# Row maxima of attention: products sent one by one, one transpose a set, rows spread through DRAM, the second set's done in the projection

## The reference

```python
q, k, v = (proj(w_q), proj(w_k), proj(w_v))        # 32 heads of 16, 4 batches of 512 tokens
scores = jnp.einsum('bhqd,bhkd->bhqk', q, k) / jnp.sqrt(jnp.float32(D_K))
attn = jax.nn.softmax(scores, axis=-1)
out = jnp.einsum('bhqk,bhkd->bhqd', attn, v)
```

## Time and profile before

| | us |
|---|---|
| median of 3 runs | 1923.91 (1920.84 to 1927.97) |
| profiled run | 1923.31 |
| its span | 1921.6 |
| mean granted clock of TensorE | 0.961 |
| projection, from the first rows gathered | about 744 to 921.6 |
| attention | 922 to 1327 |
| busy: PE, DVE, ACT, POOL | 1718.2, 1475.6, 829.8, 680.0 |

### The profile page before, as it was taken

The page is one execution under the profiler, slowest core; times in us unless marked ns, Lnnn a source line. Parts: engine busy times, 40 slices in busy tenths (PEclk is TensorE's granted clock), DMA queues, the critical chain, the costliest instruction groups (busy, mean ns, idle before and its releaser), DMA issues. The chain is left out here.

```text
span 1921.6 us, 24417 instructions
## 1 busy us (share of the span) xinstructions
PE 1718.2 (89%) x7762; PEld 1045.0 (54%) x7762; DVE 1475.6 (77%) x2715; ACT 829.8 (43%) x1415; POOL 680.0 (35%) x413
## 2 busy tenths in 40 slices
PE   8999979786959995999788888888989999999997
PEld 2333323224747873876333333334768778778786
DVE  7999999999726666753588888884976776776678
ACT  6657464444203554321477777776521111111112
POOL 5898999994234654300130000000031330330100
PEclk8999999999979997999799999999989999999999
DMA  5434344321147996864543333320010000000002
GB/s 159 122 124 119 117 129 123 91 71 39 67 185 281 414 414 244 278 213 159 138 119 91 91 93 94 94 72 4 1 67 1 33 34 1 34 33 1 1 1 88
DMA packets 111583, 213.27 MB, mean 111 GB/s; under 512 B 19012, under 2 KB 35780, under 8 KB 110554
## 3 DMA queue, kind: packets, MB, share of 16 engines
q1 hardware_dynamic: 106337, 194.94, 31.3%
q0 software_dynamic: 5120, 16.78, 2.6%
HBM read 146.85 MB, written 62.72 MB: 109 GB/s over the span
## 5 line engine op out<-in xcount | busy, mean ns | idle before, releaser
L2150 DVE TENSOR_REDUCE early_top<-att_first 128x1 f32<-128x512 f32 x480 | 311.4, 686 | 52.5 <-PE att_first L2035 45.0
L562 DVE TENSOR_TENSOR_SCAN ssm_h<-ssm_da,ssm_dbx 128x512 f32<-128x512 f32 x256 | 303.8, 1206 | 1.8 <-ACT ssm_da L441 1.5
L283 POOL TENSOR_TENSOR ssm_dbx<-ssm_u,ssm_bbc 128x2048 f32<-128x2048 f32 x63 | 285.6, 4534 | 26.2 <-DVE ssm_h L562 25.7
L2111 ACT ACTIVATE att_prob<-att_second 128x1024 f32<-128x1024 f32 x256 | 248.1, 1022 | 82.8 <-PE att_second L2055 77.7
L653 PE MATMUL ssm_y<-ssm_hc,all_ident 128*128 128x512 f32 x384 | 216.1, 646 | 42.4 <-DVE ssm_hc L528 42.4
L441 ACT ACTIVATE ssm_da<-ssm_dt,ssm_minus_a 128x512 f32<-128x512 f32 x256 | 176.6, 690 | 168.2 <-DVE ssm_h L562 168.1
L2533 ACT ACTIVATE ffn_silu<-ffn_pg 128x256 f32<-128x256 f32 x112 | 43.2, 386 | 407.1 <-PE ffn_pg L129 407.1
L2398 POOL TENSOR_TENSOR pairs_raw<-pairs_raw,pairs_scales 128x512 f32<-128x512 f32 x42 | 42.2, 1043 | 485.3 <-DMA pairs_raw<-in_w 485.3
L127 PE MATMUL ffn_pg<-pairs_wh,last_XH 128*128 128x512 f32 x448 | 176.9, 395 | 1.7 <-PEq L2201 1.7
L128 PE MATMUL ffn_pg<-pairs_wl,last_XH 128*128 128x512 f32 x448 | 176.8, 395 | 0.0
L129 PE MATMUL ffn_pg<-pairs_wh,last_XL 128*128 128x512 f32 x448 | 175.6, 392 | 0.0
(11 more groups left out here) (355 smaller groups left out, 3635.0 us busy)
## 6 DMA issues: line engine op xcount, KB each, us to landing
all_X<-in_w SPq DMA_DIRECT2D x29, 769.0 KB, 10.3
ssm_bbc<-brow_dram SPq DMA_DIRECT2D x64, 256.0 KB, 4.2
ssm_cbs<-crow_dram SPq DMA_DIRECT2D x64, 256.0 KB, 3.4
sorted_x<-ssm_zero SPq DMA_DIRECT2D x47, 256.0 KB, 3.6
sorted_y<-exp_y SPq DMA_DIRECT2D x47, 256.0 KB, 10.6
mlps_raw<-in_w SPq DMA_DIRECT2D x14, 769.0 KB, 9.5
pairs_raw<-in_w SPq DMA_DIRECT2D x7, 1536.0 KB, 6.5
v_dram<-all_sums SPq DMA_DIRECT2D x16, 512.0 KB
```

What stands on the lines that cost most here:

```text
L283: nc.gpsimd.tensor_tensor(dbx[:, n % 2], u[:, n // STATE % 2], bbc[:, n % RING, :].unsqueeze(1).to_broadcast([P, KC, NB]), ALU.mult).then_ ...
L562: nc.vector.tensor_tensor_scan(h[:, n % 2, c, :], da[:, i % 2, :], dbx[:, n % 2, c, :], 0.0, ALU.mult, ALU.add).then_inc(h_ready, 1)
L2111: nc.scalar.activation(prob[step % 2][:, js, :], p_second[second_place(step, pair) % 2][:], ACT.Exp, scale=DK ** -0.5).then_inc(exp_done, 1)
L2150: nc.vector.tensor_reduce(top[w % 2][:, qt, item:item + 1], p_first[first_place(m) % FIRSTS][:], AX.X, ALU.max).then_inc(max_done, 1)
```

## The change

Five things, all in the way of the maxima:
- *Single products.* In attention `first` sends one product, which waits for its own buffer. A step is now: product 0, `weigh`, turn, products 1 and 2, first pair of scores, product 3, second pair of scores.
- *One transpose.* `minus` is transposed as a whole, 128 x 32 to 32 x 128, and copied as such (32 x 128 instead of 8 x 512).
- *Through DRAM.* SP stores this 16 KB to `max_dram`, waits for the store, and loads it with four DMAs (two partition groups, two head pairs) into the q slot. The six loads of q for set s+4 stand between the store and the four loads; those of k and v come after.
- *Second set in the projection.* Minus after units 36 and 44, turn after units 37 and 45 in the banks of the x transposes, copy after units 38 and 46, store one unit later, the four loads another unit later (for the second set after the last store). In attention turning starts with the third set (`EARLY_SETS`). The waits for stores and loads at the end of the projection are moved to the places in attention that need them; buffers `hi` and `lo` live on and hold the output copies and two slots of v.
- *GpSimd's split* of the output weights is cut into four pieces each.

The diff, cut; left out are the counts of sets and semaphores that follow from this, and blank lines.

```diff
@@ -1461,12 +1461,19 @@
-def load_row_maxima(queue, slot, rows, done):
+def store_row_maxima(queue, g, w, rows, done):
+    queue.dma_start(g.max_dram[w % 2], rows[:].bitcast(F32)).then_inc(done, 16)
+def load_row_maxima(queue, g, slot, w, done):
+    src = g.max_dram[w % 2].rearrange("(t r) q -> r t q", r=2 * SET)
     for k in range(2):
         at = k * ROWS + TERMS
-        queue.dma_start(slot[at:at + 2 * SET, :, :].bitcast(F32),
-                        rows[:].bitcast(F32).unsqueeze(1).to_broadcast([2 * SET, PAIRS, NB])).then_inc(done, 16)
+        for pair in range(PAIRS):
+            queue.dma_start(slot[at:at + 2 * SET, pair, :].bitcast(F32).rearrange("r (t q) -> r t q", q=P), src
+                            ).then_inc(done, 16)
@@ -1569,17 +1580,21 @@
-        FIRST_UNIT, TURN_UNIT = 28, 38
+        FIRST_UNIT = 28
+        MINUS_UNIT = [FIRST_UNIT + QTILES * PAIRS * (w + 1) for w in range(2)]
+        ROWS_UNIT = [u + 2 for u in MINUS_UNIT]
...
             for kind, k in entries:
                 out.append((kind, k))
+                if kind == "unit" and k in MINUS_UNIT:
+                    out.append(("minus", MINUS_UNIT.index(k)))
+                if kind == "unit" and k - 1 in MINUS_UNIT:
+                    out.append(("turn", MINUS_UNIT.index(k - 1)))
                 if kind == "unit" and FIRST_UNIT <= k < FIRST_UNIT + f.STEPS * PAIRS:
                     out.append(("first", k - FIRST_UNIT))
-                if (kind, k) == ("unit", TURN_UNIT):
-                    out.append(("turn", 0))
@@ -1607,9 +1630,10 @@
-                if u == TURN_UNIT + 2:
-                    sp.wait_ge(rows_ready, 1)
-                    load_row_maxima(sp, f.qs[0], f.rows, f.rows_in)
+                if u - 1 in ROWS_UNIT:
+                    send_maxima(ROWS_UNIT.index(u - 1))
+                if u - 2 in ROWS_UNIT:
+                    spread_maxima(ROWS_UNIT.index(u - 2))
@@ -1627,13 +1651,10 @@
-            for k in range(2):
-                sp.wait_ge(stored[k], 16 * qk_before(len(units)))
-                sp.wait_ge(v_stored[k], 16 * TILES // 2)
-            for loaded in f.loaded:
-                sp.wait_ge(loaded, 192)
-            sp.wait_ge(f.selected, 32 * f.LOADED)
-            sp.wait_ge(f.rows_in, 32)
+            if ROWS_UNIT[1] + 1 >= len(units):
+                send_maxima(1)
+            if ROWS_UNIT[1] + 2 >= len(units):
+                spread_maxima(1)
@@ -1707,23 +1728,20 @@
-                if p == TURN_UNIT - FIRST_UNIT + 1:
-                    pe.wait_ge(rows_ready, 1)
...
-            def turn_max(_):
-                pe.wait_ge(minus_lo, 1)
-                pe.wait_ge(max_done, 2 * (TURN_UNIT - FIRST_UNIT + 1))
-                for qt in range(QTILES):
-                    mm = pe.transpose(p_first[0][0:2 * SET, qt * P:(qt + 1) * P],
-                                      minus[:, qt].rearrange("p k h -> p (k h)").bitcast(F32), g.ident[:])
-                mm.then_inc(max_turned, 1)
+            def turn_max(w):
+                pe.wait_ge(minus_lo, w + 1)
+                pe.wait_ge(xl_ready, TILES)
+                pe.transpose(pt[w][0:QTILES * 2 * SET, 0, :], minus[w][:].rearrange("p t k h -> p (t k h)").bitcast(F32),
+                             g.ident[:]).then_inc(max_turned, 1)
@@ -1771,9 +1789,10 @@
-                    if k == TURN_UNIT + 1:
-                        act.wait_ge(max_turned, 1)
-                        nc.scalar.activation(f.rows[:], p_first[0][0:2 * SET, :], ACT.Copy).then_inc(rows_ready, 1)
+                    if k in ROWS_UNIT:
+                        w = ROWS_UNIT.index(k)
+                        act.wait_ge(max_turned, w + 1)
+                        nc.scalar.activation(f.rows[w][:], pt[w][0:QTILES * 2 * SET, 0, :], ACT.Copy).then_inc(rows_ready, 1)
                     continue
@@ -1971,23 +1995,42 @@
-            slot = w % RING
             if w >= RING:
                 sp.wait_ge(pv_done, STEPS * (w - RING + 1))
-            for which, dst in enumerate((qs, ks)):
-                load_terms(sp, g, dst[slot], w, which, loaded[slot])
+            load_terms(sp, g, qs[w % RING], w, 0, loaded[w % RING])
+        def load_rest(sp, w):
+            load_terms(sp, g, ks[w % RING], w, 1, loaded[w % RING])
             load_v(sp, w)
+        def send_max(sp, w):
+            sp.wait_ge(rows_ready, turned_by(w))
+            spread(sp, w - 2)
+            store_row_maxima(sp, g, w, rows[w % 2], f.rows_out)
+        def spread(eng, w):
+            if row_loads(w):
+                eng.wait_ge(m_in[w % RING], 64 * row_loads(w))
+            else:
+                eng.wait_ge(f.rows_in[w], 64)
         def load_max(sp, w):
-            sp.wait_ge(rows_ready, w)
-            load_row_maxima(sp, qs[w % RING], rows[w % 2], m_in[w % RING])
+            sp.wait_ge(f.rows_out, 16 * (w + 1))
+            load_row_maxima(sp, g, qs[w % RING], w, m_in[w % RING])
         @block.sync
         def _(sp):
+            for k in range(2):
+                sp.wait_ge(f.v_stored[k], 16 * TILES // 2)
@@ -1996,10 +2039,14 @@
-                if s + 1 < SETS:
+                if EARLY_SETS <= s + 1 < SETS:
+                    send_max(sp, s + 1)
+                if s + RING - 1 < SETS:
+                    load(sp, s + RING - 1)
+                if EARLY_SETS <= s + 1 < SETS:
                     load_max(sp, s + 1)
                 if s + RING - 1 < SETS:
-                    load(sp, s + RING - 1)
+                    load_rest(sp, s + RING - 1)
@@ -2019,34 +2066,35 @@
-            def first(step, pair):
-                w, qt = step // STEPS, step % STEPS
-                if step % STEPS == 0 and pair == 0 and loads(w):
-                    pe.wait_ge(loaded[w % RING], 192 * loads(w))
-                for k in range(2):
-                    m = 4 * step + 2 * pair + k
-                    first_free(first_place(m))
-                for k in range(2):
-                    m = 4 * step + 2 * pair + k
-                    at = slice(k * ROWS, k * ROWS + TERMS)
-                    pe.matmul(p_first[first_place(m) % FIRSTS][:], qs[w % RING][at, pair, qt * P:(qt + 1) * P],
-                              ks[w % RING][at, pair, :], start=True, stop=True).then_inc(first_ready, 1)
...
+            def first(step, item):
+                w, qt, pair, k = step // STEPS, step % STEPS, item // 2, item % 2
+                if step % STEPS == 0 and item == 0:
+                    if loads(w):
+                        pe.wait_ge(loaded[w % RING], 192 * loads(w))
+                    else:
+                        pe.wait_ge(f.loaded[w], 192)
+                m = 4 * step + item
+                first_free(first_place(m))
+                at = slice(k * ROWS, k * ROWS + TERMS)
+                pe.matmul(p_first[first_place(m) % FIRSTS][:], qs[w % RING][at, pair, qt * P:(qt + 1) * P],
+                          ks[w % RING][at, pair, :], start=True, stop=True).then_inc(first_ready, 1)
...
             def turn_max(w):
-                pe.wait_ge(minus_lo, w)
+                pe.wait_ge(minus_lo, turned_by(w))
                 second_free(maxima_place(w))
-                for qt in range(STEPS):
-                    mm = pe.transpose(p_second[maxima_place(w) % 2][0:2 * SET, 0, qt * P:(qt + 1) * P],
-                                      minus[w % 2][:, qt].rearrange("p k h -> p (k h)").bitcast(F32), g.ident[:])
-                mm.then_inc(max_turned, 1)
+                pe.transpose(p_second[maxima_place(w) % 2][0:QTILES * 2 * SET, 0, 0:P],
+                             minus[w % 2][:].rearrange("p t k h -> p (t k h)").bitcast(F32), g.ident[:]).then_inc(max_turned, 1)
...
             def second(step, pair):
                 s, kt = step // STEPS, step % STEPS
-                if kt == 0 and pair == 0 and row_loads(s):
-                    pe.wait_ge(m_in[s % RING], 32 * row_loads(s))
+                if kt == 0 and pair == 0:
+                    spread(pe, s)
@@ -2084,16 +2132,21 @@
-                if step + LEAD < TOTAL:
+                ahead, more = step + LEAD < TOTAL, step + 1 < TOTAL
+                if ahead:
                     first(step + LEAD, 0)
                 if step:
                     weigh(step - 1)
-                if kt == 1 and s + 1 < SETS:
+                if kt == 1 and EARLY_SETS <= s + 1 < SETS:
                     turn_max(s + 1)
-                if step + LEAD < TOTAL:
+                if ahead:
                     first(step + LEAD, 1)
-                if step + 1 < TOTAL:
+                    first(step + LEAD, 2)
+                if more:
                     second(step + 1, 0)
+                if ahead:
+                    first(step + LEAD, 3)
+                if more:
                     second(step + 1, 1)
@@ -2112,11 +2165,10 @@
-                act.wait_ge(max_turned, w)
-                if w >= 3:
-                    act.wait_ge(m_in[(w - 2) % RING], 32 * row_loads(w - 2))
```

(20 more changed lines are left out.)

86 lines of the change are left out of this document (54 added, 32 removed).

## The result

| | before | after |
|---|---|---|
| median | 1924.93 us (1920.84 to 1927.97, 4 runs) | 1895.65 us (1893.78 to 1898.94, 4 runs) |
| ratio, 95% interval | | 0.9853 (0.9837 to 0.9869) |
| span of the profiled run | 1921.6 | 1892.9 |
| mean granted clock | 0.961 | 0.965 |

29 us, 1.5%, are gone; 1905 was forecast, in a range of 1886 to 1934. To see where, I cut each trace at the first exponential of a set (L2111 before, L2164 after): up to that of set 0, from there to set 3, on to set 31, and to the end.

A forecast was written before the change was run, and what follows sets the result against it. It took a loop through VectorE and TensorE in attention to set the pace. 1923.3 - 2.8 (projection) - 12.7 (start of attention) - 26 x (12.30 - 12.18) (steady sets) = 1904.7, forecast 1905 us, range 1886 to 1934.

The forecast's parts named there:

- The loop through VectorE and TensorE: Attention: maximum, freed product, V products, next product, maximum set the pace; 2.80 us per step, 12.34 per set against 12.30 seen.
- Projection, -2.8: End of the projection: 3.4 us of waiting at the transposes goes, two added transposes cost 0.3 each; sum -2.8.
- Start, -12.7: Start of attention: waits for the second set's maxima and GpSimd's subtraction go, 39.0 us become 26.3; bounds -10 to -13.
- what is late next: Start of attention, once its two waits are gone: the low clock of the first ten us (0.50), which stays.
- Steady sets, the engines: Steady attention: shorter turn (0.53 to 0.20) and 0.13 less per step from single products allow 11.5 us a set.
- Rival 3: Steady attention: splitting costs TensorE more, a set takes 12.5 or 12.6, total 1913 to 1916 us; chance 0.12.
- Steady sets, the way through DRAM: Steady attention: the maxima's detour is the wait the change adds; 4.75 + 0.60 + 6.83 makes a set 12.18 us.
- C: Steady attention: time from the maxima being copied to their use, through store and loads; 6.8 us, bounds 6.15 and 8.2.
- Rival 1: Steady attention: the way through DRAM is short enough, the loop rules at 11.5 to 11.97 a set, 1887 to 1899; chance 0.20.
- the objection that I drew from the page: Way through DRAM: two DMAs in a row at about 2.0 us fixed each, 4.0 plus issue, speak against the change.
- the forecast's case: Whole kernel: both early stages gain as summed and a steady set takes 12.18 us, giving 1905; chance 0.42.
- The chance of faster, 0.67: Whole kernel: chance of a median under 1914.3 us, mostly from the forecast's case (0.38) and Rival 1 (0.20).

The follow-up runs named there:

- weights_apart: Changed kernel with the 1 MB and 1.5 MB weight loads for GpSimd cut into 4 and 6 pieces over several sets; 1871.85 us, ratio to before 0.9838.
- after_again: The changed kernel itself, with no edit, run again beside its variants; 1899.17 us, ratio to before 0.9861.
- before_single: The kernel before, with only its first products sent singly instead of in pairs; 1915.71 us, ratio to before 0.9945.
- two_between: Changed kernel with two k loads of the later set also between the store of the maxima and their four loads; 1913.34 us, ratio to before 0.9936.
- k_between: Changed kernel with all k and v loads of the later set also between the store of the maxima and their loads; 2018.07 us, ratio to before 1.0601.
- rows_first: Changed kernel with the four loads of the maxima right behind their store, ahead of the six q loads; 1872.48 us, ratio to before 0.9833.

## Why the prediction was right, and where it was off

**What bounds the kernel: right.** The loop through VectorE and TensorE set the pace and does so still. Its terms after are 0.75 (a maximum at 1083.09, the single product whose buffer it frees at 1083.84), 1.42 (to the pair at 1085.26) and 0.53 (to the maximum at 1085.79), in sum 2.70 against 2.67 forecast: splitting took 0.09 off the first term, not 0.13.

**Projection, -2.8: -3.4 in the table.** Pairs 3.38 to 3.46 apart throughout, one of 3.52 where the first transpose is. That one costs 0.1 and not 0.3; the second lies behind the last pair, and the stretch from there to the first exponential is no longer than before (16.8 for 17.1). No switch is to be seen. Measured from the projection's first product (756.5 before, 758.0 after) to the first scores the part is 4.8 shorter, in the repeat 4.0. Of the 4.8, 1.3 lie ahead of the first pair, where the change does nothing, and stay unexplained. SP's loads cost nothing, as forecast.

**Start, -12.7: -8.9.** By the prediction's own measure, first scores to the products of the ninth step, 39.0 became 27.6 (repeat 28.2), against 26.3 with bounds of 26 to 29. The rest of the miss comes after the ninth step: the third set takes 14.2 where it had 12.3. The step that failed is the question what is late next, to which I named only the low clock. The stores of sets 2 and 3 were queued behind the weights; weights_apart and after_again show it. The signs were there: in SP's order `load_wo` stands just ahead of the sets, and the earlier trace rows has a load that took 6.2 where the median is 2.2. I used the medians. The sentence that I would be wrong altogether if the start kept a stall over 2 us was too strong: it kept one of 3.1. So was "at most one piece" for a minus that meets GpSimd's pieces: it stood through two and three of them (2.48 and 3.93). And two inputs are not needed for it: these two, and the one of 3.65 in before_single, are the TENSOR_SCALAR, which has one.

**Steady sets, the engines: nearly right.** 11.5 forecast, 11.73 measured. The turn is 0.21 (0.20 forecast). Of the 4 x 0.13 for splitting only 0.25 came: by before_single 0.09 and 0.08 in the plain step and that with the turn, but 0.04 in the step with the output's turn, where the next product waits for other maxima, and 0.02 in the one after it, which has the divide. Rival 3 is refuted: product 3 starts 0.23 after the first scores (its sign was over 0.3) and 10 ns before the scores beside it (1080.21, 1080.22). It holds half of the array and the first score the other. I had charged a slot of 0.24 for it. The Trainium skill (TensorEngine Tiling (Array Packing), Key Properties) says that different tiles work in parallel; the trace agrees, also for a matmul of 48 rows beside one of 56 (the 10 ns).

**Steady sets, the way through DRAM: the term that was mis-sized.** C was forecast at 6.8 with bounds 6.15 to 8.2, and came out at 5.9, under the lower bound. Its terms, forecast and seen (1082.94 is the copy's end):
- store issued and started 0.35: 0.38 (1083.32);
- six q loads 2.98: 2.80 (to 1086.12);
- three pitches of 0.40: 1.06 (0.35 each);
- landing and start 2.3: 1.65 (two_between: last issue at 1045.54, scores at 1047.20).

The sum is 5.89: scores could start at 1088.83, and the loop lets them start at 1088.93. The landing is over two thirds of the miss: I took that of a 64 KB load for one of 16 KB, and made the least value of those rows my bound. The store landed in 1.4, not 2.5. And the part from scores to the copy's end was 5.19 where the way is what is waited for (two_between), not 5.35, so that the way alone allows a set of 11.1. Rival 1, with 0.20, is what the steady sets did; its time, 1887 to 1899, holds the 1895.65.

By the Trainium skill (DMA: Bandwidth & Descriptors, Anatomy of one DMA) about 2.0 us are fixed for each DMA. The page gives this for DMAs that GpSimd issues, and the prediction took it for those of SP too; these, issued by SP, took 1.4 (store) and 1.65 (load, until TensorE used it). The measurement decides, and the objection that I drew from the page falls with it.

**The range held, the forecast's case did not.** The start behaved worse than forecast and the sets like rival 1. That the median came within 10 us of 1905 is in part luck: the start's shortfall of 4 hid a third of what the sets gave beyond the forecast. The chance of faster, 0.67, rested on cases that agreed in sign.

## What to carry to other kernels

A detour through DRAM costs its issues and a short landing, and while it is shorter than the loop beside it, it costs next to nothing; what counts is what else is in the queue. Here two further loads ahead of it cost 0.7%, seven cost over 7%, and a megabyte of weights ahead of it 3 us once. Before you sum up what a change removes at a place, list the large transfers that are in flight there, and take landings from rows of the same size. And leave slack: a loop 0.6 slower than its transfers gave most delays back, one at par with them kept each.

## What the runs showed of the hardware

- A VectorE minus that meets GpSimd's subtraction stands until an instruction of GpSimd ends: 4.07 with 4.52, 3.65 in before_single, 0.3 to 1.0 with pieces of 0.6 to 1.3, but 2.48 across two pieces without a gap and 3.93 across three (k_between). The Trainium skill (SBUF — State Buffer, SBUF: two separate sides) says the shared pair is held "for the whole instruction"; the rows agree, and the 2.48 and 3.93 add that the length of a piece is no upper bound.
- In k_between TensorE's waits of 3.5 to 5.4 us in each set came with a clock of 0.50, during or right after each of them. In two_between waits of 0.7 left it at 1.00; of the longer ones there, one idle time of 1.7 (1060.3) was followed by 0.50, one of 1.8 (1147.0) was not.
- How long the low clock lasts after the idle time ahead of attention differs from run to run of one kernel: until 925 in one and until 933 in the other, 3 us of the total.
- Loads of 16 KB from DRAM to 8 partitions are issued each 0.35 us, q loads of 64 KB each 0.47.
- Instruction loads share the DMA engines: near them stores landed in 1.7 to 3.2 us (1.4 otherwise) and SP's issues stalled by up to 1.5. The Trainium skill (Runtime: NRT & Kernel Launch, Instruction fetch mechanics) calls crossing such a block mostly hidden; here 8.6 us of waits fell beside them, of which the loop hid all but 0.5 to 2 us. The times coincide closely (rows_first), but that these loads are the cause was not tested.
